# Splitting the low halves of the tokenizer's waves between VectorE and GpSimd

## The reference

```python
xb = 2.0 * jnp.pi * xyz[..., None] * freq_bands          # xyz [8, 3, 512, 192], 6 bands
feat = jnp.concatenate([jnp.sin(xb), jnp.cos(xb)], axis=-1)
feat = feat.reshape(b, n, -1)                             # [8, 512, 6912]
return jnp.einsum('bnf,of->bno', feat, W)                 # W [192, 6912]
```

## Time and profile before

| | |
|---|---|
| median of 3 runs | 2548.89 us |
| the profiled execution | 2549.66 us, span 2547.8 us |
| mean granted clock of TensorE | 0.97 |
| busy TensorE | 2387.0 us (94%) |
| busy VectorE | 2040.1 us (80%) |
| busy ScalarE | 1851.1 us (73%) |
| busy GpSimd | 1285.0 us (50%) |
| L283, 48 instructions | 237.7 us, 4951 ns each |
| L267, 48 instructions | 125.5 us, 2615 ns each |
| L274, 48 instructions | 65.3 us, 1360 ns each |
| L1226, 480 instructions | 506.5 us, 1055 ns each |

### The profile page before, as it was taken

The page is one execution under the profiler, slowest core; times in us unless marked ns, Lnnn a source line. Parts: engine busy times, 40 slices in busy tenths (PEclk is TensorE's granted clock), DMA queues, the critical chain, the costliest instruction groups (busy, mean ns, idle before and its releaser), DMA issues. The chain is left out here.

```text
span 2547.8 us, 61308 instructions
## 1 busy us (share of the span) xinstructions
PE 2387.0 (94%) x21902; PEld 1690.7 (66%) x22138; DVE 2040.1 (80%) x3192; ACT 1851.1 (73%) x2913; POOL 1285.0 (50%) x1259
## 2 busy tenths in 40 slices
PE   5999999799989999999999999999999999999946
PEld 3677777666656666666666666666666666666634
DVE  7999999788868787878787878787878787878652
ACT  6777777476667777777777777777777777777641
POOL 0000000266656666666666666666666666666530
PEclk9999999799989999999999999999999999999965
DMA  6421120111100000000000000000000000000001
GB/s 139 125 56 37 39 53 19 46 45 49 44 1 2 0 0 0 0 0 0 0 0 0 0 0 0 0 0 0 0 0 0 0 0 0 0 0 0 1 7 63
DMA packets 19885, 46.35 MB, mean 18 GB/s; under 512 B 4000, under 2 KB 10400, under 8 KB 19512
## 3 DMA queue, kind: packets, MB, share of 16 engines
q1 hardware_dynamic: 18680, 45.11, 6.8%
q10 hardware_dynamic: 1152, 0.51, 0.1%
HBM read 41.67 MB, written 3.93 MB: 18 GB/s over the span
## 5 line engine op out<-in xcount | busy, mean ns | idle before, releaser
L1022 ACT ACTIVATE phi<-ps_t,betat,gt 64x512 f32<-64x512 f32 (+1 forms) x1280 | 852.1, 666 | 17.0
L1226 POOL TENSOR_TENSOR phi_lo<-phi 128x512 bf16<-128x512 f32 x480 | 506.5, 1055 | 558.9 <-ACT phi L1022 558.9
L949 PE MATMUL ps_y<-staging,o_hi 128*128 128x384 bf16 x1920 | 468.7, 326 | 21.5 <-DVE o_lo L1139 21.5
L949 PE MATMUL ps_y<-staging,o_lo 128*128 128x384 bf16 x1920 | 469.0, 326 | 0.0
L949 PE MATMUL ps_y<-wf_lo,o_hi 128*128 128x384 bf16 x1920 | 468.9, 326 | 0.0
L1218 POOL TENSOR_TENSOR q_ssq<-q_ssq,half 128x8 f32<-128x8 f32 x240 | 439.1, 1830 | 18.8
L1139 DVE TENSOR_TENSOR o_lo<-ps_u,o_hi 128x512 bf16<-128x512 f32 x240 | 164.4, 685 | 214.3 <-ACT o_hi L1032 214.3
L171 PE MATMUL acc<-w_b,feat 128*128 128x384 bf16 x1728 | 295.3, 331 | 34.8 <-ACT feat L222 28.1
L1032 ACT ACTIVATE o_hi<-ps_u 128x512 bf16<-128x512 f32 x240 | 143.5, 598 | 239.0 <-PE ps_u L935 239.0
L949 PEld LDWEIGHTS ps_y<-staging,o_lo 128*128 128x128 bf16 x1920 | 187.8, 98 | 124.2
L949 PEld LDWEIGHTS ps_y<-wf_lo,o_hi 128*128 128x128 bf16 x1920 | 187.6, 98 | 124.4
(11 more groups left out here) (213 smaller groups left out, 5391.3 us busy)
## 6 DMA issues: line engine op xcount, KB each, us to landing
xt<-in_x_dram SPq DMA_DIRECT2D x32, 320.0 KB, 5.3
wf_f<-in_wf_dram SPq DMA_DIRECT2D x24, 384.0 KB, 3.1
xt<-in_x_dram SPq DMA_DIRECT2D x32, 256.0 KB, 5.8
out_dram<-h SPq DMA_DIRECT2D x8, 480.0 KB, 4.6
staging<-in_wq_t_dram SPq DMA_DIRECT2D x1, 3072.0 KB, 12.5
staging<-in_tok_w_dram SPq DMA_DIRECT2D x8, 240.0 KB, 10.4
staging<-in_tok_w_dram SPq DMA_DIRECT2D x8, 192.0 KB, 10.3
staging<-in_kv_w_dram SPq DMA_DIRECT2D x1, 1536.0 KB, 15.7
```

The source lines that it names most:

```text
L949: last = nc.tensor.matmul(ps_y[:, n, 0:HC], lhs, w[part][:, c, n * HC:(n + 1) * HC], start=c == 0 and lhs is oh and part == 'wf_hi', stop= ...
L1022: last = nc.scalar.activation(phi[sign * DH:(sign + 1) * DH, j % 2, a:b, head, :], ps_t[rows, a * P:b * P].rearrange("p (i n) -> p i n", n ...
L1226: nc.gpsimd.tensor_tensor(phi_lo[:, j % 2, :, head], phi[:, j % 2, :, head], phi_hi[:, j % 2, :, head], ALU.subtract).then_inc(s["phi_lo_d ...
```

## The change

GpSimd subtracts the first four of the 18 slots of each step, all of them sines, and VectorE the other fourteen. GpSimd has a loop of its own over the 48 steps; it waits for the first Sin of the step and for the low products of two steps before. TensorE's low products and the reduction L267 wait for a second semaphore.

```diff
+    SHARE = 4
...
+        wave_ready, low_ready, first_low_ready = sem("wave_ready"), sem("low_ready"), sem("first_low_ready")
...
                 def multiply_low(b, p):
                     u, i = at(b, p)
+                    pe.wait_ge(first_low_ready, STEPS * b + p + 1)
                     pe.wait_ge(low_ready, STEPS * b + p + 1)
...
                         dve.wait_ge(hi_used, s - 1)
+                        dve.wait_ge(first_low_ready, s - 1)
                         dve.wait_ge(low_ready, s - 1)
...
-                    nc.vector.tensor_tensor(low[:, r], feat[:, r], high(r), ALU.subtract).then_inc(low_ready, 1)
+                    nc.vector.tensor_tensor(low[:, r, SHARE:], feat[:, r, SHARE:], high(r)[:, SHARE:],
+                                            ALU.subtract).then_inc(low_ready, 1)
...
+                def first_lows(b, p):
+                    s = STEPS * b + p
+                    r = p % RING
+                    pool.wait_ge(wave_ready, 2 * s + 1)
+                    if not (isinstance(b, int) and s < RING):
+                        pool.wait_ge(lo_used, s - 1)
+                    nc.gpsimd.tensor_tensor(low[:, r, 0:SHARE], feat[:, r, 0:SHARE], high(r)[:, 0:SHARE],
+                                            ALU.subtract).then_inc(first_low_ready, 1)
+
+                for p in range(STEPS):
+                    first_lows(0, p)
+                with pool.Fori(1, BATCH) as b:
+                    for p in range(STEPS):
+                        first_lows(b, p)
```

More of the change, by code:

```diff
@@ L82, in tokenizer @@
         rounded, reduced, cos_ready = sem("rounded"), sem("reduced"), sem("cos_ready")
-        wave_ready, low_ready = sem("wave_ready"), sem("low_ready")
+        wave_ready, low_ready, first_low_ready = sem("wave_ready"), sem("low_ready"), sem("first_low_ready")
         hi_used, lo_used = sem("hi_used"), sem("lo_used")
```

## The result

The changed kernel takes 2562.64 us, the median of six runs (2560.91 to 2562.99), against 2549.03 us of the kernel before in its own six (2547.3 to 2551.85): 13.6 us slower, a ratio of 1.0052 with a 95% interval of 1.0039 to 1.0065. Forecast were 2564.6 us in a range of 2554 to 2585.

The account below looks back on a forecast made before the run. VectorE was taken to set the tokenizer's pace, 0.27 us a step ahead of TensorE. The terms 14.6 + 1.7 - 0.6 = +15.7 us on the median 2548.9 gave 2564.6 us, range 2554 to 2585 for 8 in 10.

Parts of the forecast that it names:

- GpSimd's end after the low difference's: Tokenizer step: waiting GpSimd starts 0.14 us before the low difference's recorded end, so its 1.89 us end 1.75 us after.
- period: Tokenizer step on VectorE: from 9.01 us, or 9.26 with the add into h, to 9.43 in every step.
- first steps, to the 4th low difference: GpSimd gets in before the second half of VectorE's low halves of the weights, in two steps: +1.7 us in all.
- 43 steps: Tokenizer's steady steps: 29 at +0.42 us and 14, with the add into h, at +0.17: 14.6 us.
- end: Tokenizer's end: the last high product's slack of 0.6 us behind its Sin, held up by TensorE, goes: -0.6 us.
- how the waiting VectorE operation resumes: Reduction behind GpSimd's subtraction: ends its own time less 0.13 us after GpSimd's end, read from attention-stage line L1101.
- The two longer sums: By skill pages: GpSimd subtraction 2.25 us, sum 17 us longer; blocking until 115 ns after the other's end, 12 us more.
- Two smaller readings: Tokenizer: TensorE waits 0.6 us every step; low products of two steps before end some 0.5 us before the first Sin.
- the first (side by side): Tokenizer: GpSimd runs beside VectorE without turns, TensorE's 8.82 us a step bind: -11.2 us, 2538 us; chance 6%.
- The second (cost and saving cancel): Tokenizer: GpSimd holds VectorE only 1.1 us a step, time stays within 0.2%, 2544 to 2554 us; chance 9%.
- The third (every turn in full): Tokenizer: GpSimd comes too late, nothing overlaps: 9.98 us a step, +42 us, 2591 us; chance 7%.
- The fourth, TensorE's clock: Tokenizer: waits in every step drop TensorE's clock from 2.4 GHz to 1.2: 10.4 us a step, +57, 2606 us; chance 3%.

Follow-up runs that it names:

- e1: Changed kernel with GpSimd filling its four slots with zeros instead of subtracting, its loop written out: 2534.50 us against 2547.51 of the kernel before, ratio 0.9947.
- e6: Changed kernel with GpSimd taking two slots instead of four: 2550.23 us against 2550.74 of the kernel before, ratio 0.9998.
- e3: Changed kernel with GpSimd's subtraction waiting for the second Sin of the step instead of the first: 2572.75 us, ratio 1.0096 to the kernel before.
- e5: Changed kernel with GpSimd taking eight slots instead of four: 2600.04 us against 2550.74 of the kernel before, ratio 1.0194.

## Why the prediction was right

| step | as predicted | measured |
|---|---|---|
| low difference | 3.88 us | 3.884 |
| GpSimd's subtraction by itself | 1.89 us | 1.893 |
| GpSimd's end after the low difference's | 1.75 us | 314.29 - 312.54 = 1.75 |
| reduction's end after GpSimd's | 2.49 us | 316.71 - 314.29 = 2.42 |
| period | 9.43 us, with and without the add | 9.36, both |
| first steps, to the 4th low difference | +1.7 us | 65.12 - 63.50 = +1.62 |
| 43 steps | +14.6 us | 402.68 - 390.80 = +11.9 |
| end | -0.6 us | 13.15 - 13.50 = -0.35 |
| sum | +15.7 us | +13.15 in the traces, +13.6 in the medians |

The mechanism and its place held. In 43 steps GpSimd ended 1.75 or 1.76 us after the low difference, and the reduction 2.41 or 2.42 us after GpSimd; two of the three turns on the low halves of the weights and the one late turn in the backlog (97.40 us) were foreseen too. The term that was mis-sized is how the waiting VectorE operation resumes. It was taken as its own time less 0.13 us, from L1101; the reduction ended 2.42 us after GpSimd, 0.20 less than its 2.62. That is 0.07 us a step and 3 us over 43, about as much as their sum was too long (14.6 against 11.9). The end gave 0.35 us and not 0.6, because the last high product still starts 0.24 us after its Sin (470.28 against 467.92 + 2.12). The two longer sums that the prediction set beside its own did not come: GpSimd took 1.893 us and not 2.25, and as it ended 1.75 us after the low difference, it started before that one's recorded end, not after it.

Two smaller readings were off and cost nothing. TensorE was to wait some 0.6 us for the first Sin in each step; before its high products it waited 0.74 us (302.69), not at all (311.67) and 0.37 us (321.04) in the three steps of a half. And the low products of two steps before were to end some 0.5 us before the first Sin; in the middle one of these steps they ended 0.07 us after it (311.68 against 311.61) and released GpSimd, which stood behind the low difference until 312.54 anyway.

Of the rivals, the first (side by side) is out by L270's 4.03 us; its price was nearly that of e1, where the two do run side by side: 13.0 us faster against 11.2. The second (cost and saving cancel) did not happen at four slots, but does at two, as e6 shows. The third (every turn in full) did not come either: the low differences are 9.36 us apart and not 9.98. Even e3, which moved the turn on purpose, stayed at 25.2 us above the kernel before, below that rival's 42.

The fourth, TensorE's clock: the granted clock stayed at 1.00 over the stretch, with waits of 0.37 and 0.74 us in two steps of three. The high product that had been slow behind a wait of 2.35 us kept its speed behind a wait of 1.63:

```profile
88.26 6.03 PE L172 MATMUL acc<-w_b,feat 128*128 128x384 bf16 x36 [1.63 <-DVE h L292]
```

The add into h, for which TensorE waits there, came 1.07 us earlier in its step, as much as the low difference ahead of it is shorter. Such a fall does occur in another run. In e5, from 293 us on, one high product in three takes 7.70 us behind a wait of 2.10, and the granted clock is 0.94 between 283 and 338 us, which fits 1.2 GHz instead of 2.4 for a part of that time:

```profile
293.25 7.70 PE L172 MATMUL acc<-w_b,feat 128*128 128x384 bf16 x36 [2.10 <-ACT feat L224]
```

At 232.52 us of the same run the product behind a wait of 2.09 had kept 6.03 us, with a granted clock of 1.00 between 200 and 283 us. So the length of the wait alone does not decide, and what does stays open here. VectorE still set the pace of e5 (busy 54.39 of the 55 us).

## What to carry to other kernels

Before work goes to an engine that stands idle, look whether operations of the two engines have been seen to wait for each other: here up to 1.41 of the idle engine's 1.89 us were paid by the busy one's next operation, more than the 1.07 us that the move saved. The trace had shown it in another stage, as an operation that takes 0.68 or 1.53 us by what GpSimd does. Such a wait is no gap in a timeline; it is a longer duration, so compare minimum and maximum of one instruction. A small piece that fits the pause between two dependent operations is nearly free: 256 elements gained 5.5 us, 512 nothing, 1024 lost 13.6 and 2048 lost 49.3.

## What the runs showed of the hardware beyond that

The sign bit has one input, runs at 0.59 ns an element, and takes turns with GpSimd all the same: 2.93 us for 1.36 in e3. With it even a write has to wait. The fill of e1 takes 0.95 us alone (its minimum) and ends 0.89 us after the sign bit's end whenever it comes while that runs (312.59 + 1.91 = 314.50 against 313.61), while beside the two-input low difference it goes on undisturbed. The other order is there once: the fill of 83.27 us came before the sign bit, which started at 83.68, took 1.75 us for its 1.36 and ended 1.21 us after the fill. So in these runs the two-input operations took turns with GpSimd's reads only, the sign bit with its writes as well; why an operation with one input does so, no run here shows. A VectorE operation that had to wait is also left with less than its own time: 2.42 us for 2.62, and in e3 too 1.21 for 1.36 (GpSimd ends at 314.18, the sign bit at 315.39).
